# Odd x blocks turned by VectorE instead of TensorE, in a convolution with routed low-rank experts on Trainium2

## The reference, cut to what matters

```python
u_m = u * mask[:, None, :]
k_f = jnp.fft.rfft(kernel, n=n)
u_f = jnp.fft.rfft(u_m, n=n)
y = jnp.fft.irfft(u_f * k_f, n=n)[..., :Lq]
y = (y + u_m * D[:, None]) * mask[:, None, :]
...
logits = jnp.einsum('bsd,ed->bse', y, route_w)
topk_v, topk_idx = jax.lax.top_k(logits, 1)
route_weight = jax.nn.one_hot(topk_idx[..., 0], E) * topk_v
h = jnp.einsum('bsd,erd->bser', y, A)
out = x + jnp.einsum('bser,eor->bso', route_weight[..., None] * h, Bw)
```

## Time and profile before

| | |
|---|---|
| time, median of 3 runs | 616.39 us (616.24 to 616.44) |
| the profiled execution | 616.44 us, span of the core 614.6 us |
| PE busy | 587.9 us (96%), 3681 matmuls |
| DVE / POOL / ACT busy | 481.1 (78%) / 385.9 (63%) / 327.5 us (53%) |
| granted TensorE clock | full in all 40 slices |
| transfers | 77.65 MB in 37071 packets, 126 GB/s |

### The profile page before, as it was taken

The page is one execution under the profiler, slowest core; times in us unless marked ns, Lnnn a source line. Parts: engine busy times, 40 slices in busy tenths (PEclk is TensorE's granted clock), DMA queues, the critical chain, the costliest instruction groups (busy, mean ns, idle before and its releaser), DMA issues.

```text
span 614.6 us, 13508 instructions
## 1 busy us (share of the span) xinstructions
PE 587.9 (96%) x3681; PEld 532.4 (87%) x3681; DVE 481.1 (78%) x1305; ACT 327.5 (53%) x1123; POOL 385.9 (63%) x520
## 2 busy tenths in 40 slices
PE   3579999999999999999999999999999999999996
PEld 3468899899989989998998999999899999989984
DVE  7678778787877878787787888777777877777875
ACT  3677664556456455545645554564555456455420
POOL 4667756666675666667566667757566775665430
PEclk9999999999999999999999999999999999999999
DMA  6113344345344434433443453454454344344422
GB/s 128 63 53 100 135 153 137 106 147 154 96 138 155 125 115 149 153 97 139 154 115 125 149 149 100 141 155 112 125 152 142 103 144 155 102 134 153 132 85 86
DMA packets 37071, 77.65 MB, mean 126 GB/s; under 512 B 11836, under 2 KB 20350, under 8 KB 36998
## 3 DMA queue, kind: packets, MB, share of 16 engines
q1 hardware_dynamic: 27846, 43.76, 28.0%
q10 hardware_dynamic: 9152, 33.03, 13.2%
HBM read 43.16 MB, written 33.62 MB: 125 GB/s over the span
## 4 chain that ended last, share of the span: by engine, by line
PE 92%; DVE 4%; ACT 2%; issue 1%; POOL 1%; DMA 0%; ACTq 0%; POOLq 0%; DVEq 0%
PE psYo L1062 19%; PE psZ L1084 19%; PE psO L1062 15%; PE psYe L1062 13%; PE psS L1062 11%; PE psO L1111 5%; PE psXe L1073 4%; PE psXo L1073 4%; PE psZ L1150 1%; PE psS L1123 1%; DVE psS L931 0%; DVE ex L773 0%; DMA logs<-in_L_cond_log_dt_dram 0%; POOL both L469 0%; DVE ost L963 0%
## 5 line engine op out<-in xcount | busy, mean ns | idle before, releaser
L508 POOL TENSOR_TENSOR Slo<-Sf,Shi 128x384 fp32r<-128x384 f32 x64 | 65.4, 1021 | 172.5 <-ACT Shi L661 172.5
L931 DVE SCALAR_TENSOR_TENSOR psS<-Sf,tab,psS 64x128 f32<-64x128 f32 x256 | 91.9, 359 | 50.2 <-ACT Sf L656 42.7
L1084 PE MATMUL psZ<-Wt,Y 128*128 128x136 f32 x1024 | 129.2, 279 | 0.0
L1084 PEld LDWEIGHTS psZ<-Wt,Y 128*128 128x128 f32 x1024 | 123.3, 190 | 0.1
L656 ACT ACTIVATE Sf<-psS 128x128 f32<-128x128 f32 x64 | 17.8, 277 | 193.1 <-PE psS L1062 192.9
L963 DVE TENSOR_TENSOR ost<-psO,xt 128x512 f32<-128x512 f32 x128 | 88.4, 691 | 1.7 <-PE psO L1062 1.1
L501 POOL TENSOR_TENSOR Xlo<-xeven,Xhi 128x512 fp32r<-128x512 f32 x64 | 82.4, 1287 | 0.0
L469 POOL TENSOR_TENSOR both<-coarse,fine 128x512 f32<-128x512 f32 x64 | 68.8, 1075 | 1.3 <-ACT fine L595 1.2
L947 DVE TENSOR_TENSOR wlo<-psZ,whi 128x128 fp32r<-128x128 f32 x64 | 18.7, 292 | 55.5 <-ACT whi L666 55.5
L1062 PE MATMUL psO<-Bw_hi,whi 128*128 128x512 f32 x128 | 50.4, 394 | 0.7 <-ACT whi L666 0.7
L1062 PE MATMUL psYo<-Xlo,Thi 128*128 128x512 f32 x128 | 50.8, 397 | 0.0
(11 more groups left out here) (197 smaller groups left out, 1541.4 us busy)
## 6 DMA issues: line engine op xcount, KB each, us to landing
xt<-in_x_dram SPq DMA_DIRECT2D x64, 512.0 KB, 4.9
out_dram<-ost ACTq DMA_DIRECT2D x63, 512.0 KB, 5.2
Traw<-kdram SPq DMA_DIRECT2D x64, 128.0 KB, 2.9
kdram<-krow SPq DMA_DIRECT2D x64, 1.0 KB
A_nat<-in_L_ffn_A_dram SPq DMA_DIRECT2D x1, 512.0 KB, 5.1
B_nat<-in_L_ffn_Bw_dram SPq DMA_DIRECT2D x8, 64.0 KB, 3.5
out_dram<-ost SPq DMA_DIRECT2D x2, 256.0 KB, 2.0
lens_i<-in_itok_B_dram SPq DMA_DIRECT2D x1, 64.0 KB, 4.2
```

What stands on the lines that cost most here:

```text
L508: pool.tensor_tensor(Slo[h.s2][:, :], Sf[h.s2][:, :], Shi[h.s2][:, :].bitcast(F32), ALU.subtract).then_inc(slo_done, 1)
L931: dve.scalar_tensor_tensor(psS[to, new], Sf[h.s2][fr, old], tab2[fr, BR, h.n:h.n + 1], psS[to, new], ALU.mult, ALU.add).then_inc(brought_d ...
L1084: last = pe.matmul(psZ[:, 0:NW], Y[:, j, c, :], Wt[:, 2 * c + j, :], start=(j == 0 and c == 0), stop=(j == 1 and c == NE - 1), skip_group_ ...
```

## The change

The odd blocks are no longer turned by PE. They are read from memory a second time, in 16 small transfers per head, into a tile `xblk` in which every group of 32 partitions holds the four 32-row groups of x for 32 positions; one VectorE transpose of 128 x 512 elements, which turns each 32 x 32 square by itself, then gives the turned odd blocks in `xodd`. A small transfer moves 32 x 4 runs of 32 numbers (128 bytes), 16 KB in all; the runs lie 256 KB apart in memory (one batch row of x). Eleven of the 16 are issued by SP, five by ACT; the first heads differ. `load_x` of a head is issued before its small transfers.

`x_hi_odd` copies `xodd` on ACT, `x_lo_odd` subtracts on POOL, where DVE did it before. `turn_blocks(1)` stands at the start of the DVE step, ahead of `carry`; `x_hi_odd(1)` on ACT behind `first_state`; `x_lo_odd(1)` on POOL between `g_table` and `s_lo`. `skew_kernel` moves from the end of a step on SP to the start of the next, which leaves its place in the queue's order the same. In the opening, PE turns the second table (`pack2`) ahead of Bw instead of behind it.

```diff
+        xblk = [sb(f"xblk{s}", [P, NE, G4, G32]) for s in range(2)]
+        xodd = sb("xodd", [P, HALF])
...
+        PIECES = [(g, c) for g in range(G4) for c in range(NE)]
+
+        def load_blocks(eng, h, pieces):
+
+            need(eng, xodd_done, h.n - 1)
+            for g, c in pieces:
+                eng.dma_start(xblk[h.s2][g * G32:(g + 1) * G32, c, :, :],
+                              bass.AP(x.tensor, h.n * L + c * Q + P + g * G32,
+                                      [[H * L, G32], [G32 * H * L, G4], [1, G32]])
+                              ).then_inc(blk_in[h.s2], 16)
...
             def step(head):
+                if head(1).there and not is_head(head(0), 1):
+                    skew_kernel(head(1))
                 if head(2).there:
                     load_x(head(2))
+                    load_blocks(sp, head(2), PIECES[:11])
                     write_kernel(head(2))
-                    skew_kernel(head(2))
...
+            load_blocks(sp, Head(0), PIECES[:8])
...
             load_x(Head(1))
+            load_blocks(sp, Head(1), PIECES)
             load_x(Head(2))
             sp.wait_ge(pad_done, 32)
             for n in range(3):
                 write_kernel(Head(n))
                 skew_kernel(Head(n))
+                if n == 1:
+                    load_blocks(sp, Head(2), PIECES)
...
+            def x_lo_odd(h):
+
+                need(pool, xhi_odd, h.n + 1)
+                need(pool, y_mm, (h.n - 1) * 2)
+                pool.tensor_tensor(Xlo[h.s2][:, 1, :], xodd[:, :], Xhi[h.s2][:, 1, :].bitcast(F32),
+                                   ALU.subtract).then_inc(xlo_odd, 1)
...
+                if head(1).there:
+                    x_lo_odd(head(1))
                 if head(0).there:
                     s_lo(head(0))
                 if head(1).there:
...
             g_table(first[0])
+            x_lo_odd(first[0])
             g_table(first[1])
             g_lo(first[0])
             g_table(first[2])
             angle_steps(parts[1])
             t_lo(first[0])
             g_lo(first[1])
+            x_lo_odd(first[1])
             s_lo(first[0])
             x_lo(first[1])
...
+            load_blocks(act, Head(0), PIECES[8:])
...
-            def x_hi(h, j):
-                need(act, xt_done, h.n * 2 + j + 1)
+            def x_hi_even(h):
+                need(act, xt_done, h.n + 1)
                 need(act, y_mm, (h.n - 1) * 2)
-                act.activation(eo(Xhi[h.s2], j), psX[j][:, :], ACT.Copy).then_inc(xhi_done, 1)
+                act.activation(eo(Xhi[h.s2], 0), psX[0][:, :], ACT.Copy).then_inc(xhi_even, 1)
+
+            def x_hi_odd(h):
+                need(act, xodd_done, h.n + 1)
+                need(act, y_mm, (h.n - 1) * 2)
+                act.activation(eo(Xhi[h.s2], 1), xodd[:, :], ACT.Copy).then_inc(xhi_odd, 1)
...
             def step(head):
+                if head(2).there:
+                    load_blocks(act, head(2), PIECES[11:])
                 if head(-2).there:
                     store(head(-2))
                 if head(0).there:
                     first_state(head(0))
+                if head(1).there:
+                    x_hi_odd(head(1))
                 if head(3).there:
                     m_matrix(head(3))
                 if head(1).there:
-                    x_hi(head(1), 0)
-                    x_hi(head(1), 1)
+                    x_hi_even(head(1))
...
-            def x_lo(h):
-
-                need(dve, xhi_done, h.n * 2 + 2)
-                need(dve, y_mm, (h.n - 1) * 2)
-                dve.tensor_tensor(eo(Xlo[h.s2], 1), psX[1][:, :], eo(Xhi[h.s2], 1).bitcast(F32),
-                                  ALU.subtract).then_inc(xlo_odd, 1)
+            def turn_blocks(h):
+
+                need(dve, blk_in[h.s2], (h.half + 1) * 16 * G4 * NE)
+                need(dve, xlo_odd, h.n)
+                dve.transpose(xodd[:, :], xblk[h.s2][:, :, :, :].rearrange("p c g i -> p (c g i)")
+                              ).then_inc(xodd_done, 1)
...
             def step(head):
+                if head(1).there:
+                    turn_blocks(head(1))
                 if head(0).there:
                     carry(head(0))
-                if head(1).there:
-                    x_lo(head(1))
                 if head(-1).there:
                     largest(head(-1))
...
-            def turn_x(h, j):
+            def turn_x(h):
 
                 need(pe, x_in[h.s4], h.quarter * 16 + 16)
-                need(pe, *((xlo_odd, h.n) if j else (xeven_done, h.n)))
+                need(pe, xeven_done, h.n)
                 for c in range(NE):
-                    at = (2 * c + j) * P
-                    last = pe.transpose(psX[j][:, c * P:(c + 1) * P], xt[h.s4][:, at:at + P], ident[:, :])
+                    at = 2 * c * P
+                    last = pe.transpose(psX[0][:, c * P:(c + 1) * P], xt[h.s4][:, at:at + P], ident[:, :])
                 last.then_inc(xt_done, 1)
...
-                need(pe, xhi_done, h.n * 2 + 2)
+                need(pe, xhi_even, h.n + 1)
+                need(pe, xhi_odd, h.n + 1)
                 need(pe, xlo_even, h.n + 1)
                 need(pe, xlo_odd, h.n + 1)
...
                     bring(head(0))
                 if head(1).there:
-                    turn_x(head(1), 0)
-                    turn_x(head(1), 1)
+                    turn_x(head(1))
...
+            pe.wait_ge(pack2_done, 2)
+            pe.wait_ge(xeven_done, 1)
+            turn_tables(pack2, psX[0], 5)
             pe.wait_ge(in_B, 16 * E)
...
-            pe.wait_ge(pack2_done, 2)
-            pe.wait_ge(xeven_done, 1)
-            turn_tables(pack2, psX[0], 5)
             inputs(first[0])
             turn_k(first[0])
             bring(first[0])
-            turn_x(first[1], 0)
-            turn_x(first[1], 1)
+            turn_x(first[1])
```

More of the change, by code:

```diff
@@ L40, in conv_ffn_kernel @@
     G16 = 16
+    G32 = 32
+    G4 = P // G32
     assert B == P and 2 * N == P and ER == P and HALF == 512 and H % 8 == 0
@@ L231, in conv_ffn_kernel @@
         xt_done = sem("xt_done")
-        xhi_done = sem("xhi_done")
+        blk_in = [sem(f"blk_in{s}") for s in range(2)]
+        xodd_done = sem("xodd_done")
+        xhi_even = sem("xhi_even")
+        xhi_odd = sem("xhi_odd")
         xeven_done = sem("xeven_done")
@@ L703, in _ @@
             first = [Head(n) for n in range(4)]
-            x_hi(first[0], 0)
-            x_hi(first[0], 1)
+            x_hi_even(first[0])
             x_even(first[0])
@@ L726, in _ @@
             m_matrix(first[0])
+            x_hi_odd(first[0])
             for j in range(2):
@@ L736, in _ @@
             first_state(first[0])
-            x_hi(first[1], 0)
-            x_hi(first[1], 1)
+            x_hi_odd(first[1])
+            x_hi_even(first[1])
             b_hi(first[1])
@@ L1026, in masks @@
                        ALU.is_gt).then_inc(mask_done, 1)
-            x_lo(first[0])
+            turn_blocks(first[0])
             dve.wait_ge(in_len, 16)
@@ L1038, in _ @@
             masks(0, 4)
+            turn_blocks(first[1])
             dve.wait_ge(tab_done, 2)
             carry(first[0])
-            x_lo(first[1])
             b_lo(first[1])
@@ L1195, in _ @@
             pe.wait_ge(consts, 9)
-            turn_x(first[0], 0)
-            turn_x(first[0], 1)
+            turn_x(first[0])
             pe.wait_ge(pack1_done, 1)
```

## The result

The changed kernel is slower: 628.45 us median (625.0 to 630.1, 4 runs) against 616.41 of before on the same chip, a ratio of 1.019, with a 95% interval of 1.0145 to 1.0232. Forecast were 606. The profiled execution took 628.9 us, its span is 627.1.

A forecast was written before the change was run, and what follows sets the result against it. The prediction took PE to set the pace, busy 72 of 72 us. Its terms summed as -26.7 + 15.1 + 1.3 = -10.3 from 616.4, about 606 us; range 592 to 632, the forecast alone 601 to 612.

The forecast's parts named there:

- SP. Eleven issues, 11 x 0.32 = 3.5 us: SP between load_x and write_kernel: issues fit into its 5.8 us wait for krow, hidden up to 0.5 us each.
- PE's 26.7 us: PE loses psXo's four transposes: 0.43 us saved in each of 62 steps.
- rival 1: Covers are longer than they look and PE simply gets faster: 591 us, range 590 to 600, chance 0.14.
- The stalls: 14 steps each: from_states waits 0.45 us behind fractions and clamp, up waits 0.24 and 0.39 with turns and mirror.
- the upper case of that step: DVE behind fractions and clamp: if frac waits for Grev, carry is 1.05 us late and the stall 0.8.
- The transpose: New DVE transpose ahead of carry: taken as 0.70 us, between 0.52 and 1.37; free in ordinary steps with 0.80 idle.
- rival 2: DVE transpose is long and carry pays every step: slower, about 638 us at 1.37 us, chance 0.20.
- The opening: POOL's opening list gets x_lo_odd twice, once ahead of head 0's Slo: between nothing and 2 x 1.29, taken as 1.3 us.
- The runs: Small transfers, 2048 runs of 128 bytes a head: 15 ns a run, 1.9 us a step, fitting into 8.56.
- Rival 3: Small runs are too slow and DVE waits for blk_in: 871 us at 72 ns a run, 698 at 50; chance 0.10.
- The pieces' landing: If the pieces land behind x, which takes 4.9 us, they are there some 2 us before the next step's transpose.
- ACT's five issues: Head of ACT's step, ahead of store and Sf: 1.6 us at 0.32 each, hidden up to 0.5 us each.

The follow-up runs named there:

- without loads: Changed kernel with the small loads of heads 2 to 63 left out, all computing and other transfers kept: 606.95 us, 0.984.
- without loads and with the stalls moved away: Changed kernel without small loads of heads 2 to 63, turns and mirror behind k_row, fractions and clamp behind carry one step later: 591.89 us, 0.9604.
- The third buffer: Changed kernel with xblk three times instead of twice, the pieces loaded a step earlier: 632.7 us, 1.0266.
- 761 us: Changed kernel with load_x and four pieces issued on SP ahead of skew_kernel, so Traw stands behind them: 760.87 us, 1.2335.
- the run with three pieces in the wait: Changed kernel with three of SP's eleven pieces issued behind the kernel row, ahead of Traw, the other eight behind x: 612.04 us, 0.9927.

## Why the prediction was wrong, step by step

- **The step that failed** is "SP. Eleven issues, 11 x 0.32 = 3.5 us, [...] Hidden up to 0.5 us each". The mechanism stood there, but the term and its cover were both mis-sized. The eleven issues took 6.3 us with their gaps, 0.57 each.
  The cover was larger than the 5.8 us in the text: SP also waited 73.3 / 60 = 1.2 us a step for the adds, so a step of 8.49 left 5.8 + 1.2 - 0.4 = 6.6 us, or 0.60 an issue. By this sum (an estimate; no run changed the parts singly) the issues alone would just have fitted.
  What took SP's step past the pace is that with them the kernel row's landing was waited for 1.36 us instead of 0.85, and x's issue took up to 0.60 instead of 0.33; the prediction put both growths at nothing.
  I took 0.32 from Traw, which SP issues alone after a wait; an issue in a train is another thing. The rows ahead of the prediction have no train, but the trace of before has one, in the opening, of eight issues with 1024 runs each, 0.85 us apiece:

```profile
5.01 6.80 SPq L373 DMA_DIRECT2D B_nat<-in_L_ffn_Bw_dram  x8
```

  That would have been a bound from above, 11 x 0.85 = 9.4 us, beyond the cover. I should have kept the term open up to it, added SP's step up from row to row, and made it a rival that ends slower. The rivals had transfers that are slow, but no queue that is. That 628 us lies within 592 to 632 is luck: the upper end stood for a slow transpose.
  The Trainium skill (DMA: Bandwidth & Descriptors, Issuing engines are not separate DMA queues) says that issuing on several engines saves only the time to initiate a transfer, usually small against the transfer. For one piece that holds here, 0.57 us against 2.8 to landing. But landings overlap and issues on a queue don't, so eleven of them are 6.2 us of a 9.3 us step.
- **What it cost.** Steps of 9.10 us against 8.75 without loads (whi from 48.0 to 599.2 in 63 steps) are 0.35 x 63 = 22 us, and 628.45 - 606.95 is 21.5. The forecast's other terms came together to 606.95 against 606, as a sum in which small misses cancel.
- **PE's 26.7 us** were real but for 1.5: without loads and with the stalls moved away the step is (583.6 - 46.8) / 63 = 8.52 us, against 8.92 - 0.43 = 8.49, and 0.40 x 63 is 25.2. The 591.89 us of that run are rival 1's 591, with its condition met by hand. That they agree so closely is in part luck, since its opening is not 1.3 us longer, but 46.8 us against 46.9.
- **The stalls,** 14 x (0.45 + 0.24 + 0.39) = 15.1 us, came to 15.1 as a difference of two medians. In the two profiled executions 14.4 us lie in the 63 steps, and the opening differs by 1.2 (48.0 against 46.8). From start to start on PE (means of 55 and 57 steps, times four), the run without loads spends 0.47 us more ahead of from_states than the one with the moves (0.45 forecast), 0.47 around up (0.24 + 0.39 forecast), and 0.16 ahead of turn_wh, which had no term. In the run without loads the two frac take 0.89 us under Grev, near the upper case of that step:

```profile
306.69 0.89 DVE L915 SCALAR_TENSOR_TENSOR frac<-step_l,frac 128x64 f32<-128x64 f32 x2
306.71 0.79 POOL L500 TENSOR_TENSOR Grev<-both 128x256 f32<-128x256 f32 x1
```

- **The transpose** lasts 708 ns against 0.70; rival 2 falls. ACT's copy is 630 ns, within its 0.70. The opening is 48.0 - 46.9 = 1.1 us later, against 1.3.
- **The runs** of 128 bytes: SP's queue took 0.372 x 16 x 627.1 = 3732 us of engine time against 0.280 x 16 x 614.6 = 2753, so 979 us more for 711 x 128 runs, 10.8 ns each; ACT's, by the same sum, 648 us for 313 x 128, 16 ns, or 12.4 over both (an estimate: the whole growth is put down to the pieces). I had 15. Rival 3 falls: the pitch of 256 KB and 8 MB costs nothing like 36 ns a run.
- **The pieces' landing** "some 2 us before the next step's transpose" did not hold (19.4 us of waits), since the last piece is issued some 6 us later than x and not 3.5. The third buffer shows that it set nothing.
- **ACT's five issues** were hidden as said, though at 454 ns each: ACT still waits for PE ahead of Sf, 184.4 us in 57 times, against 188.0 in 60.

## What to carry to other kernels

Count a queue that only issues as an engine: add up its whole step, the waits that it must sit out included, and set it against the pace; its slack, which is the sum of its waits for others and not the longest alone, is used up as busy time is. Waits for landings can grow with the traffic. Take the price of an issue from a train of issues under traffic, not from a lone one, and look for time in which the queue waits on a landing, for that is where issues cost nothing. And a wait placed ahead of an urgent transfer can close a loop through four engines, as 761 us showed.

## What the runs showed of the hardware that was not expected

- A small transfer's issue took 0.31 us straight behind the kernel row's and 0.43 behind another piece's (medians of the run with three pieces in the wait), and up to 0.88 for some behind x, whether it carried 128 runs or 32 (1.26 and 1.25 us for three), as a pattern of two dimensions or three (433 ns both); Traw alone takes 0.32 to 0.34. With gaps, that is 0.55 to 0.61 in a long train. An issue by ACT at the same time is not what lengthens them: in the changed kernel, 60 to 564 us, SP's 194 pieces that overlap one take 0.46 us in the mean, the 409 others 0.56.
- A float32 transpose of 128 x 512 on VectorE takes 697 to 715 ns in all 64 cases, while two frac that take 0.57 us in the earlier trace rows take 0.89 when they start with Grev, and 0.35 where POOL does nothing beside them (the run without loads and with the moves, at 301.97).
